# A transformer block on one core: the first batch's stack DMAs issued from other engines, and idle TensorE matmuls in the first batch

## The reference

```python
def attn(x, w_in, b_in, w_out, b_out):       # 16 heads of 16
    x_proj = (x @ w_in.T + b_in).reshape(b, l, h, -1)
    q, k, v = jnp.split(x_proj, 3, axis=-1)
    att = jnp.einsum('blhd,bmhd->blmh', q, k) * scale
    att = jax.nn.softmax(att, axis=2)
    opt = jnp.einsum('blmh,blhd->blhd', att, v).reshape(b, l, d)
    return opt @ w_out.T + b_out
def ffn(x, ...):                             # 8 experts, LoRA rank 4, F = 1024
    top1 = jnp.argmax(jax.nn.softmax(x @ gate_W.T + gate_b, axis=-1), axis=-1)
    base = x @ wi_W.T + wi_b
    out = sum over i of (top1 == i) * (relu(base + lora_i(x)) @ wo_W.T + wo_b)
x = x + layernorm(attn(layernorm(x)))
x = x + layernorm(ffn(layernorm(x)))
```

## Time and profile before

| | us |
|---|---|
| median of 3 runs | 588.12 (587.3 to 591.47) |
| profiled execution | 588.17 |
| its span, first to last instruction | 586.4 |
| TensorE, VectorE, ScalarE, GpSimd busy | 516.0, 482.0, 468.0, 213.5 |

### The profile page before, as it was taken

The page is one execution under the profiler, slowest core; times in us unless marked ns, Lnnn a source line. Parts: engine busy times, 40 slices in busy tenths (PEclk is TensorE's granted clock), DMA queues, the critical chain, the costliest instruction groups (busy, mean ns, idle before and its releaser), DMA issues.

```text
span 586.4 us, 8522 instructions
## 1 busy us (share of the span) xinstructions
PE 516.0 (88%) x2640; PEld 411.7 (70%) x2640; DVE 482.0 (82%) x1021; ACT 468.0 (80%) x1252; POOL 213.5 (36%) x382
## 2 busy tenths in 40 slices
PE   2758898898999999999999899999999999895894
PEld 2635365647778777787779677877878767685784
DVE  5478989898998999889998999899988897745333
ACT  2468999899998899889998999899988998731220
POOL 8393014402440264215721383027511542153321
PEclk9958679879999999999999999999999988998998
DMA  7294522052405222522323250523052210010011
GB/s 252 73 236 120 144 73 73 15 129 72 108 0 145 73 72 73 132 68 53 109 60 84 73 144 15 130 73 94 14 144 73 65 44 1 1 37 0 1 37 36
DMA packets 22260, 46.16 MB, mean 79 GB/s; under 512 B 5077, under 2 KB 13397, under 8 KB 21592
## 3 DMA queue, kind: packets, MB, share of 16 engines
q1 hardware_dynamic: 21592, 44.77, 28.7%
q10 hardware_dynamic: 624, 0.85, 0.4%
HBM read 7.85 MB, written 4.19 MB: 21 GB/s over the span
## 4 chain that ended last, share of the span: by engine, by line
PE 42%; DVE 24%; ACT 22%; POOL 6%; issue 2%; DMA 2%; SPq 1%; ACTq 0%; POOLq 0%; DVEq 0%
PE pu L165 22%; ACT ps L382 16%; DVE nmax L532 12%; PE ps L182 9%; DVE st L562 5%; PE ps L165 4%; POOL y L754 3%; DVE inter L558 2%; POOL nmr L748 2%; ACT inter L445 2%; DVE mv L567 2%; PE pu L187 1%; PE pu L273 1%; ACT vo L402 1%; DVE qk L546 1%
## 5 line engine op out<-in xcount | busy, mean ns | idle before, releaser
L382 ACT ACTIVATE ps<-ps,nmax 128x512 f32<-128x512 f32 x512 | 342.2, 684 | 14.2 <-DVE nmax L532 13.7
L532 DVE TENSOR_REDUCE nmax<-ps 128x1 f32<-128x512 f32 x512 | 322.9, 682 | 32.0 <-PE ps L182 30.8
L182 PE MATMUL ps<-stack 128*128 128x512 f32 x512 | 194.3, 452 | 25.8 <-ACT ps L382 21.0
L182 PEld LDWEIGHTS ps<-stack 128*128 128x128 f32 x512 | 97.4, 201 | 73.3 <-ACT ps L382 54.3
L382 ACT ACTIVATION_READ_ACCUMULATOR ps<-ps,nmax 128x1 f32 x512 | 118.2, 231 | 0.0
L165 PE MATMUL pu<-yT,wi_r 128*128 128x512 f32 x336 | 88.8, 399 | 6.1 <-DVE inter L558 4.8
L165 PE MATMUL pu<-wo_r,inter 128*128 128x256 f32 x624 | 86.1, 289 | 0.0
L165 PEld LDWEIGHTS pu<-wo_r,inter 128*128 128x128 f32 x624 | 82.5, 194 | 5.1 <-DVE qk L546 1.4
L165 PEld LDWEIGHTS pu<-yT,wi_r 128*128 128x128 f32 x336 | 62.0, 188 | 22.9 <-DVE inter L558 6.4
L768 POOL TENSOR_TENSOR ml<-gs,g 128x128 f32<-128x128 f32 x8 | 3.3, 414 | 147.3 <-DVE g L649 147.3
L745 POOL TENSOR_SCALAR nmr<-mv 128x4 f32<-128x4 f32 (+1 forms) x34 | 8.1, 239 | 133.1 <-DVE mv L567 132.4
(11 more groups left out here) (117 smaller groups left out, 601.2 us busy)
## 6 DMA issues: line engine op xcount, KB each, us to landing
stack<-qk SPq DMA_DIRECT2D x248, 128.0 KB, 2.5
xb<-in_x SPq DMA_DIRECT2D x7, 512.0 KB, 3.6
out_y<-xb SPq DMA_DIRECT2D x7, 512.0 KB, 3.0
xb<-in_wo SPq DMA_DIRECT2D x1, 1024.0 KB, 7.6
vo<-in_wi SPq DMA_DIRECT2D x2, 512.0 KB, 6.9
stack<-qk SPq DMA_DIRECT2D x12, 64.0 KB, 2.0
xb<-in_x SPq DMA_DIRECT2D x4, 128.0 KB, 4.0
oT<-in_wqk ACTq DMA_DIRECT2D x1, 512.0 KB, 4.0
```

The source lines that it names most:

```text
L182: e.matmul(ps[i % NS][:], st[:, 1 - p, c, t * 128:(t + 1) * 128], st[:, 2, c, :], start=True, stop=True).then_inc(scored, 1)
L382: e.activation(ps[i % NS][:], ps[i % NS][:], ACT.Exp, bias=nmax[:, i % 8:i % 8 + 1], accum_out=ssum[:, b % 2, t, h:h + 1]).then_inc(exped, 1)
L532: e.tensor_reduce(nmax[:, i % 8:i % 8 + 1], ps[i % NS][:], AX_X, ALU.max, negate=True).then_inc(maxed, 1)
```

## The change

The first piece's parity 1 is issued by GpSimd for both halves c: (0, 1) is taken from ScalarE, and (1, 1) from SyncE. Its semaphores are split by parity. TensorE gets matmuls whose result is never read (`run_idle`: ones times ones, 128x512 into a score bank that the next score overwrites): 25 ahead of the first transposes, 6 ahead of the first q_k, 4 ahead of pair 0, and in batch 0 one ahead of each score matmul of pairs 2 to 33, but not in the slots of `FULL`. That makes 22 slots with two each, 44. They stand behind the score's wait for its bank and, in the first pair of a piece, behind the wait for the piece.

```diff
+IDLE, FULL = (25, 6, 4), (8, 9, 13, 14, 15, 16, 27, 28, 29, 30)
...
-        first_stacked = [sem(f"first_stacked{c}") for c in range(2)]
+        first_stacked = [[sem(f"first_stacked{c}_{p}") for p in range(2)] for c in range(2)]
...
-                            qk[p:128:8, qa:ka + 1:ka - qa, c].bitcast(F32)).then_inc(first_stacked[c], 16)
+                            qk[p:128:8, qa:ka + 1:ka - qa, c].bitcast(F32)).then_inc(first_stacked[c][p], 16)
...
+            def run_idle(bank, n):
+
+                for _ in range(n):
+                    e.matmul(bank[:].rearrange("p (k m) -> p k m", k=4), ones_r[:],
+                             ones_r[:].unsqueeze(1).to_broadcast([128, 4, 128]), start=True, stop=True)
...
                 if g in (0, 4):
-                    e.wait_ge(first_stacked[c], 128)
+                    e.wait_ge(first_stacked[c][0], 64)
+                    e.wait_ge(first_stacked[c][1], 64)
                 elif g % 8 == 0:
                     e.wait_ge(stacked[piece % PIECES], pieces_at(piece))
                 for p in range(2):
                     i = 2 * g + p
                     if i >= NS:
                         e.wait_ge(exped, i - NS + 1)
+                    if 2 <= g < PAIRS + 2 and g - 2 not in FULL:
+                        run_idle(ps[i % NS], 1)
...
+            e.wait_ge(const_set, 1)
+            run_idle(ps[0], IDLE[0])
             e.wait_ge(id_loaded, 16)
...
+            run_idle(ps[0], IDLE[1])
             e.wait_ge(qk_split, 3)
             q_k(0, 0), q_k(0, 2), q_k(0, 1), q_k(0, 3)
...
             for t in ALL:
                 value(0, t)
+            run_idle(ps[0], IDLE[2])
             pair(0), pair(1)
...
             q_k(0, 0), q_k(0, 2)
-            first_piece(e, 0, 1)
             q_k(0, 1), q_k(0, 3)
...
-            e.wait_ge(qk_low, 4)
+            first_piece(e, 0, 1)
+            first_piece(e, 1, 1)
             late_halves(0, [(wi_r[:, :, 0, half(i)], wi_st[:, half(i)]) for i in range(2)], wi_loaded, 16)
...
             first_piece(e, 0, 0)
             first_piece(e, 1, 0)
-            first_piece(e, 1, 1)
             e.wait_ge(late, 4)
```

## The result

The changed kernel takes 582.32 us (median of 7 runs, 581.0 to 583.54) against 587.3 for the kernel before (7 runs, 585.29 to 591.47). The ratio is 0.9917, 95% interval 0.9897 to 0.9938: faster by 5.0 us, of which the interval leaves 3.6 to 6.0. The forecast was 586.2 with a range down to 583.0, so it had the sign but missed the size, and the range missed too. The forecast was counted from 588.17; the seven runs of the kernel before have a median of 587.3, 0.9 lower. The profiled execution took 582.15 (span 580.3) against 588.17 (586.4).

What follows compares the result with a forecast made beforehand. No single engine bounds the kernel; ScalarE's waits in the first batch's exponentials (clock 0.72) leave some 7 us. Terms -0.35 + 1.0 - 1.25 - 1.35 = -1.95 take 588.17 to 586.2 us, range 583.0 to 590.3.

Steps and rivals of the forecast that it cites:

- the price of an issue on GpSimd: First-piece DMAs: 1.0 us per GpSimd issue, taken between 0.59 and 1.5, putting late 4 at 28.64.
- The term, -0.35 in the sum: Way to piece 1: SyncE sends wi, lora and pieces 1 and 2 0.35 us earlier than at 28.98.
- Rival 1: First-piece issues: GpSimd as cheap as SyncE, 0.59 to 0.75 us, piece 1 3.3 us earlier, 583.2 us; chance 0.17.
- The head: Before the first exponential: 25 idles end near 8.2, first copy at 14.25, first exponential moves from 26.22 to about 23.9.
- The idles behind piece 1: Pairs 8 and 9 at half clock: first exponential 0.43 us later, next three 0.2 each, cost 1.0 (0 to 1.0).
- The clock in the slots: Batch 0's thinly used stretches: idles keep the clock at 1.00, saving 1.25 us (q/k projection) and 1.35 (value projections).
- Rival 3: Slots of batch 0: the clock falls in spite of the idles, 3 us lost, 591.8 us; chance 0.08.
- That it all goes through to the end: From 81.7 on the schedule is unchanged and bound by busy engines, so the whole -1.95 us reaches the end.
- Rival 2: First-piece issues: slower GpSimd issues become the chain to piece 1; at 1.5 us each 590.2 us; chance 0.17.
- break-even: GpSimd's chain to piece 1: whole kernel unchanged with late 4 at 30.6, 1.24 us per issue.
- Rival 4: First batch's exponentials: the change does not act, VectorE takes over as the bound, 588 us; chance 0.08.
- The port rule: First-piece issues: VectorE holds GpSimd's descriptor port, at most 2.2 us, 588.4 us; 5 in 100.

Runs made afterwards that it cites:

- e8: Changed kernel with all 16 first-piece DMAs issued by GpSimd and none by SyncE: 586.94 us, ratio 0.998 to the kernel before.
- e1: Changed kernel without any idle matmul, the issuing change alone: 587.06 us, ratio 0.9986 to the kernel before.
- e4: Changed kernel without the head's idle matmuls, keeping the 44 in the slots: 586.58 us, ratio 0.9968 to the kernel before.
- e3: Changed kernel without the slots' idle matmuls, keeping the 35 of the head: 584.13 us, ratio 0.993 to the kernel before.
- e5: Changed kernel without the four idle matmuls of pairs 8 and 9: 582.51 us, ratio 0.9902 to the kernel before.
- e2: Changed kernel with the first piece issued by ScalarE and SyncE as before, idle matmuls alone: 586.55 us, ratio 0.9969 to the kernel before.
- e6: Changed kernel with SyncE issuing piece 1's eight DMAs before its wait for late 4 and the wi and lora loads: 582.07 us, ratio 0.9901.
- e11: The kernel of e6 once more, no further edit: 581.89 us, ratio 0.9905 to the kernel before.
- e7: The changed kernel once more, no edit: 582.8 us, ratio 0.9913 to the kernel before.

## Why the prediction was wrong

**The failed step is the price of an issue on GpSimd.** The prediction took 1.0 us and measured is 0.51; and SyncE's 0.59, which it took for the price from below, was no floor. Eight issues at 1.0 gave `late` 4 at 28.64; it came at 25.5. The rest of that chain held: `qk_low` 4 at 19.6 as predicted (GpSimd's second four start at 19.91), casts of 3.64, and the distance from first issue to landing, 9.53 for the 9.7 assumed. The term, -0.35 in the sum, measured -3.86 at piece 1's landing: -3.43 up to `wi`'s load, -0.26 since that issue took 0.34 and not 0.59 us, -0.17 in the transfer. Rival 1 comes nearest (GpSimd as cheap as SyncE, though at 0.59 to 0.75); its 583.2 is 0.9 above the median and 1.1 above the profiled execution. It got 17 in 100 because I argued from GpSimd's slowness at data work to its DMA issues, and the rows of the changed kernel and of e8 show that the one does not price the other: 0.51 us an issue beside 1.25 for one of the subtractions that follow (2.51 for two), still below SyncE's and ScalarE's issues.

**The head** came as predicted: first copy 14.11 (14.25), first exponential 23.34 (23.9). The 25 idles ended at 9.4 and not at 8.2: they took 8.43 us, so by the prediction's own prices some 13 of them, not 8, ran at half clock (an estimate from 0.43 and 0.22). They cost the first transpose 0.3 us, which the spare time behind it took up. What I did not know is that this head varies without idles: e1 and e4 show the second projection at half clock too, 2.5 and 2.3 us from copy to copy where the kernel before had 1.5. By e3 against e1 the head's idles are worth 2.7 us at `wi`'s load and 3.1 at piece 1, more than the 1.9 that the prediction gave them at the second low half. Part of the surplus is that e1's head was colder than that of the kernel before: its second copy came 0.9 us later (18.28 against 17.36).

**The idles behind piece 1** cost what they were said to: 0.42 and three times 0.19 by the rows, 0.98 by e5 against the changed kernel.

**The clock in the slots** stayed at 1.00 from 42 to 94. The waits of 1.52 and 1.36 went, 2.88 for the 2.6 predicted. e3 shows both waits and the half clock back without the slots' idles. Rival 3, the clock falling in spite of them, did not happen in batch 0.

**That it all goes through to the end** held in the changed kernel: -5.58 at the end of batch 0, -6.1 at the end of the span. Summed with what was measured, -3.86 + 1.0 - 2.88 = -5.74. Rival 2's mechanism is real (e8), but its break-even lies at 1.24 us per issue. Rival 4 fell with the waits: the stretch got 2.6 us shorter, with VectorE busy 47.4 of its 52.9 us. The port rule of the Trainium skill ("SBUF - State Buffer", SBUF: two separate sides) can make GpSimd's issues wait for VectorE. That did not happen: the dearest of eight took 0.74 and sixteen in a row 8.16, so at most some 0.2 us was lost. Whether VectorE's operations beside them were of the kinds that the rule names, no run here tells. The Trainium skill also gives a GpSimd-issued DMA a later first byte ("DMA: Bandwidth & Descriptors", Latency and other measured facts). No run here times a first byte; the landings show no penalty: a median of 2.2 us for GpSimd's and 2.5 for SyncE's in the changed kernel, 2.0 for SyncE's in the kernel before, 1.9 for GpSimd's sixteen in e8.

**The range** failed in part for the same reason: its low end was rival 1's point value, with nothing for the smaller terms that could go further. The measured 582.3 lies 0.7 beyond it. Counted from the 587.3 of the seven runs and not from 588.17, the range would have reached down to 582.1 and taken it in. So the miss of the range hangs on the starting value; the miss of the gain, 5.0 us for the forecast 1.95, does not.

**What stays open.** The parts alone don't add up in time: e1 and e2 give 0.14% and 0.31% where both together give 0.83%. At piece 1 it is the same: 1.0 us alone each, 3.4 together. The traces explain most of it: alone, each part leaves the other's limit standing (e2: SyncE busy until 28.2 with `late` 4 met at 26.0), and e1 has a colder head. Part goes with the places where the clock falls in batch 1 and the last batch: without an edit there, batch 1 took between 54.7 and 56.4 us and the last between 58.9 and 61.6. It varies between executions of one kernel too: e6 and e11 are the same and have 61.6 and 58.9 in the last batch, the changed kernel and e7 have 55.1 and 54.7 in batch 1. So an end-to-end difference of 2 us between two single traces says little; those at piece 1 and end 0 are read at the place where the edit acts. What places the falls stays open.

## What to carry to other kernels

A DMA's issue on GpSimd is not priced like GpSimd's arithmetic; where no row shows it, set the lower bound below the cheapest engine's, count what stands behind the issues, and give the case "as cheap as elsewhere" more than the 17 in 100 that it had here, since the whole chain hangs on the price times the number of issues. A stall on one piece of data is worth following back through all queues that it crosses: here q/k copy, GpSimd issues, casts, SyncE's order, eight DMAs. And idle matmuls pay where TensorE's half clock delays real work that others wait for, and cost about a microsecond right behind a wait (e5), where TensorE comes back at half clock and each idle stands ahead of the first results.

## What was not expected of the hardware

- An issue of a 64 KB DMA from SBUF to SBUF took 0.50 us on GpSimd (16 in 8.16 us), 0.59 on SyncE and 0.67 on ScalarE.
- The granted-clock rows read 1.00 through the head even where the durations are those of half clock: in e1 the second projection took 2.5 us under a row of 1.00.
- Falls of the clock of one length came with different times of the last batch, according to where they began. In the kernel before, half clock from 480 to 487 began 28 us into the last batch (452.15), and it took 58.9 us, no more than where there was no fall; e5, from 475 to 482 and also 28 us in, has 58.9 too. In e6 a fall as long, from 477 on and 34 us in (443.19), came with 61.6. In e2 and e4 it began 28 us in and lasted 10 us, with 60.5.
- One of SyncE's issues in the first piece took 1.5 us in some executions: 1532 ns in e2 and 1515 in e7, against 633 at most in the changed kernel's first trace.
